# A decoder layer on one Trainium2 core: which engine writes the early norms of the context stage

## What is computed

```python
def _layernorm(x, axis=-1, eps=1e-05):
    m = jnp.mean(x, axis=axis, keepdims=True)
    v = jnp.var(x, axis=axis, keepdims=True)
    return (x - m) / jnp.sqrt(v + eps)
...
x = _layernorm(x + attn(x, ...))
# context experts: Wg = Wu = Wd = ctx_2048, one of E = 4 by token id
g = silu(x @ Wg[e].T); u = x @ Wu[e].T; y = (g * u) @ Wd[e].T
x = _layernorm(x + y)
# router and experts: the top 2 of 16 by x @ gate_w.T + bias, and one shared expert
x = _layernorm(x + ffn(x, ...))
```

## Time and profile before

| | us |
|---|---|
| median of three runs | 656.95 |
| lowest and highest of the three | 655.68 and 661.49 |
| the profiled execution, its own time | 655.56 |
| its span, first to last instruction | 653.8 |
| PE busy in the span | 624.3 (95%) |
| DVE, POOL, ACT busy | 534.0, 464.8, 452.6 |
| mean granted TensorE clock, of 1 | 0.991 |

### The profile page before, as it was taken

How to read it: one execution, slowest core, us unless ns; L and a number is a source line. 1 busy time by engine, 2 the same in 40 slices (tenths; PEclk the granted TensorE clock), 3 DMA queues, 4 the chain that set the end, 5 groups by cost and what they waited for, 6 DMA issues and landing times.

```text
span 653.8 us, 12044 instructions
## 1 busy us (share of the span) xinstructions
PE 624.3 (95%) x3545; PEld 491.2 (75%) x3545; DVE 534.0 (82%) x870; ACT 452.6 (69%) x742; POOL 464.8 (71%) x443
## 2 busy tenths in 40 slices
PE   7989999999999999999999999999999999899990
PEld 6677888878888788888888888878889777655550
DVE  6999999999999999999999999975974556742245
ACT  3768788797887978879788797886422445533365
POOL 4396989879898798987988878767761581545554
PEclk9999999999999999999999999999999999999996
DMA  4261113111121111311113112132025278168745
GB/s 164 76 261 60 66 50 113 54 59 64 49 113 64 49 64 49 113 64 49 64 49 113 64 49 68 44 129 90 31 76 129 79 197 343 48 189 254 197 131 153
DMA packets 25993, 66.66 MB, mean 102 GB/s; under 512 B 4099, under 2 KB 16899, under 8 KB 23179
## 3 DMA queue, kind: packets, MB, share of 16 engines
q1 hardware_dynamic: 23131, 58.54, 26.4%
q0 software_dynamic: 2832, 7.75, 4.5%
HBM read 58.00 MB, written 9.85 MB: 104 GB/s over the span
## 4 chain that ended last, share of the span: by engine, by line
PE 85%; DVE 5%; POOL 3%; ACT 3%; issue 2%; DMA 1%; ACTq 0%; DVEq 0%
PE ps L871 37%; PE ps L885 9%; PE ps L901 7%; PE ps L1165 5%; PE ps L886 4%; DVE conv L1730 4%; PE ps L803 3%; PE ps L821 3%; PE ps L1214 3%; PE ps L845 2%; PE ps L1155 1%; PE ps L910 1%; PE ps L911 1%; POOL conv L675 1%; PE ps L1210 1%
## 5 line engine op out<-in xcount | busy, mean ns | idle before, releaser
L1730 DVE SCALAR_TENSOR_TENSOR conv<-ps,w_raw,conv 128x506 f32<-128x506 f32 (+3 forms) x352 | 320.4, 933 | 14.7 <-ACT conv L1373 8.4
L871 PE MATMUL ps<-x_hi,w_hi 128*128 128x512 f32 x384 | 158.2, 412 | 2.5 <-DVE x_lo L1651 1.4
L1373 ACT ACTIVATE conv<-ps,w_raw 128x512 f32<-128x512 f32 x160 | 108.2, 687 | 63.8 <-PE ps L871 63.4
L871 PE MATMUL ps<-x_hi,w_lo 128*128 128x512 f32 x384 | 151.3, 394 | 0.0
L871 PE MATMUL ps<-x_lo,w_hi 128*128 128x512 f32 x384 | 149.9, 390 | 0.0
L532 POOL TENSOR_TENSOR decay<-cum_b,cum_tok 128x512 f32<-128x512 f32 (+1 forms) x128 | 103.2, 828 | 9.2 <-DMA cum_b<-cum_scratch 9.2
L871 PEld LDWEIGHTS ps<-x_hi,w_hi 128*128 128x128 f32 x384 | 72.2, 188 | 20.5 <-issue 2.4
L538 POOL TENSOR_TENSOR decay<-decay,mask 128x512 f32<-128x512 f32 x64 | 82.7, 1292 | 5.0
L871 PEld LDWEIGHTS ps<-x_hi,w_lo 128*128 128x128 f32 x384 | 72.0, 188 | 16.9 <-DVE w_lo L1656 0.2
L871 PEld LDWEIGHTS ps<-x_lo,w_hi 128*128 128x128 f32 x384 | 72.4, 189 | 12.7
L1358 ACT ACTIVATE conv<-conv 128x1024 f32<-128x1024 f32 x80 | 79.3, 1059 | 1.5 <-DVE conv L1730 1.5
(11 more groups left out here) (289 smaller groups left out, 1079.9 us busy)
## 6 DMA issues: line engine op xcount, KB each, us to landing
cum_b<-cum_scratch SPq DMA_DIRECT2D x16, 1024.0 KB, 4.6
w_raw<-in_winT SPq DMA_DIRECT2D x15, 778.0 KB, 4.3
y_all<-in_wgu SPq DMA_DIRECT2D x4, 1408.0 KB, 12.6
late<-in_wdn SPq DMA_DIRECT2D x2, 1408.0 KB
x_scratch<-conv SPq DMA_DIRECT2D x19, 128.0 KB, 4.6
late<-in_woutT SPq DMA_DIRECT2D x1, 2048.0 KB, 8.2
ys_scratch<-y_blk SPq DMA_DIRECT2D x32, 64.0 KB
res_scratch<-conv SPq DMA_DIRECT2D x11, 130.0 KB
```

Source lines behind the costliest of these rows:

```text
L871: mm = pe.matmul(ps[:, tile_bank(n, tile) + hf, :], wp[:, par, w], xp[:, kk, t], start=(i == 0), stop=(i == 5))
L1373: act.activation(conv[:, par, tile, hf * 512:(hf + 1) * 512], ps[:, tile_bank(n, tile) + hf, :], ACT.Copy, scale=w_raw[:, par, tap:tap + 1 ...
L1730: dve.scalar_tensor_tensor(out=o[:, :, s:], in0=u[:, :, 0:T - s], scalar=w_raw[:, par, c:c + 1], in1=o[:, :, s:], op0=ALU.mult, op1=ALU.ad ...
```

## The change

Two edits. First, who writes the early norms: POOL keeps blocks 0 and 2, both behind its first chain of roots; DVE takes blocks 1 and 3 in the round `j == EARLY` (8), behind the sum of block 6, and blocks 4 to 7 in the round `j == TBS` (11), behind the sum of block 9 and ahead of the sum of block 10. Second, ACT's copy of turned blocks 6 and 7, `take_x2(3)`, moves from behind the load of the silu table and `silu_gate(1)` to ahead of them.

```diff
-EARLY_P = 6
+POOL_NORMS, DVE_NORMS = (0, 2), (1, 3, 4, 5, 6, 7)
...
         def normed(j):
-            if j < EARLY_P:
-                return S["n1p"], j + 1
-            return S["n1"], j + 1 - EARLY_P
+            if j in POOL_NORMS:
+                return S["n1p"], POOL_NORMS.index(j) + 1
+            return S["n1"], (DVE_NORMS.index(j) if j < EARLY else len(DVE_NORMS) + j - EARLY) + 1
...
-                for j in range(g.start, min(g.stop, EARLY_P)):
+                for j in POOL_NORMS if c == 0 else ():
                     pool.tensor_scalar(xg[:, j, :], xg[:, j, :], ln_m2[:, j, 0:1], root[:, j:j + 1],
                                        ALU.subtract, ALU.mult).then_inc(S["n1p"], 1)
...
+            take_x2(3)
             act.preload_act_table_set("silu_and_others")
             silu_gate(1)
-            take_x2(3)
             take_hidden(0)
...
+            def early_norms(lo, hi):
+
+                dve.wait_ge(S["p_root"], 13 if hi == 2 else 26)
+                for j in DVE_NORMS[lo:hi]:
+                    dve.tensor_scalar(xg[:, j, :], xg[:, j, :], ln_m2[:, j, 0:1], root[:, j:j + 1],
+                                      ALU.subtract, ALU.mult).then_inc(S["n1"], 1)
+
             for j in range(TBS + 2):
...
                 if j in (EARLY // 2 + 1, EARLY + 1):
                     first_roots((j - 1) // (EARLY // 2) - 1)
-            dve.wait_ge(S["p_root"], 26)
-            for j in range(EARLY_P, EARLY):
-                dve.tensor_scalar(xg[:, j, :], xg[:, j, :], ln_m2[:, j, 0:1], root[:, j:j + 1],
-                                  ALU.subtract, ALU.mult).then_inc(S["n1"], 1)
+                if j == EARLY:
+                    early_norms(0, 2)
+                if j == TBS:
+                    early_norms(2, len(DVE_NORMS))
```

## The result

In 21 runs of each on one chip the change took 655.4 us at the median (653.44 to 657.15) and the kernel before 657.79 (655.68 to 662.63). The ratio is 0.9952 with a 95% interval of 0.9934 to 0.9969: 3.2 us less, between 2.0 and 4.3 (the medians differ by 2.4). That is a real gain, and inside the 1% that the prediction called no change. On a second chip the same pair gave 0.9946 (0.9923 to 0.9969).

A forecast was written before the change was run, and what follows sets the result against it. PE, busy 95% of the span, was taken as the bound, so only its waits could go: 0.70 + 0.82 + 0.66 = 2.2 less 0.5 = 1.7 us. 655.56 - 1.7 = 653.9 profiled, 654.6 for new runs; range 652.2 to 658.0.

The forecast's parts named there:

- Blocks 1 and 3 on DVE: At turn_x2(0): DVE norms hidden in its wait ahead of block 9's gate, removing PE's wait at block 1; 0.70 us.
- Blocks 4 to 7: At turn_x2(2): four DVE norms done before PE wants block 5, so PE's wait there goes; 0.82 us.
- ACT's copy: At router(3): copy of turned blocks 6 and 7 ahead of the table load removes PE's wait; 0.66 us.
- The new wait at ranks: At ranks: ACT's queue, then DVE's choice of experts, makes PE wait about 0.4 us; 0.5 us taken off the gain.
- To the end: Behind ranks: everything shifts as a block, nothing is lost, and the 1.7 us gain stays.
- taken up behind: Rival, behind ranks: gathers, stores or shared expert wait for something unmoved; gain 0 to 0.9 us, 655.1; chance 0.18.
- no wait at ranks: Rival, at ranks: ACT or DVE is nimbler, PE does not wait; 2.2 us gained, 653.4; chance 0.08.
- The port: DVE norms of blocks 1 and 3 beside POOL's: shared port pair might block them; forecast took no cost.
- Norms in turn: Rival, early norms: DVE's wait for both of POOL's on the port; about 1.0 us gained, 654.6; chance 0.07.
- port fight: Rival, early norms: sharing the port stretches POOL's norms to 1.98 us each; 1.1 us slower, 656.7; chance 0.05.
- The single time, 654.6: Whole kernel: time in us forecast for new runs, between 653.9 on the profiled execution and 655.25 on the median.
- New runs should fall between: Whole kernel: new runs expected between the forecasts for the profiled execution, 653.9, and the median, 655.25; hence 654.6 us.

The follow-up runs named there:

- logits_first: The change with ACT's take_logits(0, EARLY) moved ahead of take_hidden(0); ratio 0.9952 against the kernel before, median 653.79 us.
- norms_only: The kernel before with the new split of the norms but ACT's old order, take_x2(3) behind the table load; ratio 1.0032 against the kernel before.

## Why the prediction was right, step by step

- **Blocks 1 and 3 on DVE, 0.70 us.** ctx_hidden(10) started 1.15 us behind turn_x2(0) before and 0.43 after: 0.72. The norms were hidden as written, though 0.86 us long and not 0.70.
- **Blocks 4 to 7, 0.82 us.** gate_up(1) started 9.76 behind turn_x2(0) before (538.46) and 8.17 after: 1.59 together with the first, so 0.87. The added wait for 26 links cost nothing: the chain ended at 535.3, DVE came to it at 535.83.
- **ACT's copy, 0.66 us.** router(3) came at 13.50 before and 11.30 after: 2.20 in all, as forecast, and 0.61 for this step.
- **The new wait at ranks.** It is there, for the reason given (ACT's queue, then DVE). The term was too large: 0.5 us forecast (0.4 of waiting at ranks and 0.1 for router(4), held by ACT), 0.32 of waiting measured and router(4) not held. The logits copy came 1.87 earlier, not 1.7. That is 0.18 of the 0.27 us between 1.7 and 1.97. The other 0.09 is PE's: it came to gate_up(3) 2.29 us earlier (18.34 and 16.05 behind turn_x2(0)) and not 2.2, since router(3) took 0.91 us to the next step behind its wait and takes 0.81 without it. The forecast had such a cost of restarting for the other two waits and left it out here.
- **To the end.** 1.9 us are left at the first expert block, so nothing was lost behind ranks, as forecast; "taken up behind" did not happen, nor did "no wait at ranks".
- **The port.** "Norms in turn" and "port fight" did not happen: DVE's pair started 0.04 us ahead of POOL's two and neither was held for a whole instruction. The Trainium skill ("SBUF — State Buffer", the section on the two separate sides) ties its lock to a DVE operation in a two-port mode or with two SBUF inputs; it says that TENSOR_SCALAR can enter such a mode if its operands meet conditions, which the prediction left out. The lock did not show for these norms; for an operation with two SBUF inputs the trace is in line with it, with 0.48 instead of 0.29 us in logits_first.
- **What the forecast left out.** It compared one execution with another and called the rest scatter. On the runs the ratio says 3.2 us (2.0 to 4.3), and 1.7 lies below that interval. Part of the scatter goes with the three waits that this change removes: with them more runs have a low clock.
- **The single time, 654.6.** It came 0.8 under the median of 655.4, and that is partly luck. The forecast took the median before as 656.95; in the longer comparison it was 657.79, 0.84 higher. The medians differ by 2.39 us, 0.69 more than 1.7. These two errors nearly cancel; 657.79 - 1.7 would have been 656.1. What is left is the step that failed, "New runs should fall between" the profiled execution and the median (653.9 and 655.25), which took off 0.65: 8 of the 21 runs did.

## What to carry to other kernels

Removing one of several waits on the same chain can lengthen the next one: the first edit alone merged the savings into a single wait of 1.13 us, and in the profiled execution the clock then fell and the kernel was slower than before. So price edits that hang together as one, ask how long the longest single wait becomes, and read the granted clock behind it. And line up a stage by its own first instruction before spans are compared: 0.5 us between the spans were 1.97 in the stage.

## What I had not expected of the hardware

- After 1.13 us of PE idle in one piece in norms_only the clock was at its lower level from about 543.6 to 553.9, and 3.8 us were lost by ranks; 1.2 us of useless matmuls in the same place kept it at 1.00. Seven of nine runs of norms_only had a mean clock below 0.985 (0.981 to 0.984). The waits of 0.45 to 0.60 us before were passed at full clock in all three profiles that have them, and the wait of 1.58 us at 570 in nine of ten, so no single length decides.
- A DVE instruction with two SBUF inputs that starts while POOL works can be held by it (0.48 instead of 0.29 us, ending 0.14 behind POOL's). In logits_first this took away 0.19 of the 0.26 us that the logits copy had been brought forward.
